# Graph attention, Mamba and relation stages: relation rows, x1, x3 and the routing in another order

## What is computed

```
x = x + attention(layernorm(x), adj)        # masked softmax over s1[i] + s2[j], leaky relu
x = x + mamba2(layernorm(x))                # W_in, conv of 4 taps, 8 heads, W_out, W_lin
x = x + relation(layernorm(x), adj)         # sum over r of (adj == r) @ x @ weight[r], r = 1..4
x = x + moe(layernorm(x))                   # 8 experts, top 1, capacity 1.25 T / E, in token order
```

## Time and profile before

| | |
|---|---|
| median of 3 runs | 3693.07 us (3690.87 to 3696.62) |
| profiled execution | 3692.86 us, span 3691.1 us |
| busy, share of the span | PE 94%, DVE 69%, ACT 47%, POOL 49% |
| mean granted clock of PE | 0.985 of full |
| 100 to 2580 us (rounds) | PE busy 2311.57 us, DVE 1979.52, ACT 1378.12, POOL 1242.03 |
| 2660 to 3691 us (experts) | PE busy 1014.32 us of 1031 |

### The profile page before, as it was taken

The page is one execution under the profiler, slowest core; times in us unless marked ns, Lnnn a source line. Parts: engine busy times, 40 slices in busy tenths (PEclk is TensorE's granted clock), DMA queues, the critical chain, the costliest instruction groups (busy, mean ns, idle before and its releaser), DMA issues.

```text
span 3691.1 us, 63266 instructions
## 1 busy us (share of the span) xinstructions
PE 3452.6 (94%) x19340; PEld 2780.1 (75%) x19340; DVE 2537.9 (69%) x7375; ACT 1743.9 (47%) x3691; POOL 1807.0 (49%) x2010
## 2 busy tenths in 40 slices
PE   7999999999999999999999999999699999999998
PEld 6777777777777777777777777767488888888887
DVE  4877878787787878878778778787444444444444
ACT  3555555565565555556555555555223232323232
POOL 2455545445455454554545455454345454545453
PEclk8999999999999999999999999999799999999999
DMA  3111211111121111111112121111155555555553
GB/s 118 38 39 46 36 36 40 43 37 41 42 37 38 40 40 37 46 37 37 40 37 42 35 49 35 36 40 33 51 191 198 193 197 193 196 194 195 195 194 129
DMA packets 168177, 304.60 MB, mean 83 GB/s; under 512 B 38016, under 2 KB 140416, under 8 KB 149952
## 3 DMA queue, kind: packets, MB, share of 16 engines
q0 software_dynamic: 38272, 196.98, 15.4%
q1 hardware_dynamic: 92896, 72.41, 6.4%
q10 hardware_dynamic: 36960, 34.62, 6.2%
HBM read 250.77 MB, written 53.17 MB: 82 GB/s over the span
## 4 chain that ended last, share of the span: by engine, by line
PE 53%; DVE 25%; POOL 12%; issue 9%; ACT 1%; DVEq 0%; DMA 0%; ACTq 0%; POOLq 0%; SPq 0%
PE bank L1398 13%; PE bank L1412 13%; PE bank L1133 7%; POOL masks L482 6%; DVE conv L827 6%; PE bank L1149 5%; PE bank L1237 4%; PE bank L1350 4%; DVE y L1009 3%; POOL row L468 2%; DVE y L1014 2%; POOL rstd L468 2%; DVE stats L808 2%; DVE xn L818 1%; PE bank L1268 1%
## 5 line engine op out<-in xcount | busy, mean ns | idle before, releaser
L748 ACT ACTIVATE decay<-bank,w_up 128x256 f32<-128x256 f32 x568 | 268.8, 473 | 699.9 <-PE bank L1398 699.9
L1133 PE MATMUL bank<-xn1T,w_in 128*128 128x256 f32 x2304 | 524.9, 381 | 11.2 <-issue 9.4
L1149 PE MATMUL bank<-w_rel,hT 128*128 128x264 f32 x2048 | 506.7, 391 | 0.0
L1398 PE MATMUL bank<-zs,w_up 128*128 128x256 f32 x2272 | 503.5, 380 | 0.6 <-ACT zs L607 0.6
L1412 PE MATMUL bank<-w_dn,decay 128*128 128x256 f32 x2272 | 502.1, 379 | 0.0
L1133 PEld LDWEIGHTS bank<-xn1T,w_in 128*128 128x128 f32 x2304 | 431.6, 190 | 71.9 <-issue 12.0
L827 DVE SCALAR_TENSOR_TENSOR conv<-bank,conv_w,conv 128x255 f32<-128x255 f32 (+2 forms) x960 | 461.2, 480 | 34.8
L1398 PEld LDWEIGHTS bank<-zs,w_up 128*128 128x128 f32 x2272 | 432.7, 190 | 60.0 <-issue 0.9
L1412 PEld LDWEIGHTS bank<-w_dn,decay 128*128 128x128 f32 x2272 | 426.2, 190 | 55.1
L1081 DVE TENSOR_TENSOR hT<-bank,w_dn 128x256 f32<-128x256 f32 x142 | 60.3, 425 | 535.9 <-PE bank L1412 535.9
L1149 PEld LDWEIGHTS bank<-w_rel,hT 128*128 128x128 f32 x2048 | 369.2, 190 | 73.3 <-ACT hT L607 13.0
(11 more groups left out here) (238 smaller groups left out, 6189.7 us busy)
## 6 DMA issues: line engine op xcount, KB each, us to landing
token_rows<-row SPq DMA_DIRECT2D x64, 266.0 KB, 2.8
xT_sb<-in_xT ACTq DMA_DIRECT2D x64, 256.0 KB
x_sb<-in_x ACTq DMA_DIRECT2D x64, 256.0 KB, 2.7
adj_sb<-in_adj SPq DMA_DIRECT2D x64, 256.0 KB, 3.0
adjt_sb<-in_adjT SPq DMA_DIRECT2D x64, 256.0 KB, 3.0
out<-row SPq DMA_DIRECT2D x64, 256.0 KB, 2.2
w_in<-token_rows,idc POOLq DMA_INDIRECT x142, 4.7
out<-hT,ids POOLq DMA_INDIRECT x142, 2.4
```

Of the source, the lines that this page charges most:

```text
L748: nc.scalar.activation(hid(f), bank[f % 4][:, 0:GROUP], ACT.Relu, bias=b1[q % 2][:, f:f + 1]).then_inc(hid_ready, 1)
L1133: ins = mm(dst, w_in[:, k, first:first + P], xn1T[:, k, :], start=k == 0, stop=k == DK - 1)
L1149: ins = mm(bank[6 + t][:, 0:GX], hT[:, d, r * N + t * P:r * N + (t + 1) * P], w_rel[:, r, d, :], start=r == 0 and d == 0, stop=r == R - 1 ...
L1398: ins = mm(bank[f % 4][:, 0:GROUP], w1[i][:, k, f * P:(f + 1) * P], xgT[:, k, :], start=k == 0, stop=k == DK - 1)
```

## The change

Five things are done, all in the rounds.

1. PE: for t = 1, only the third relation stays ahead of L1333, behind `expo` of heads 4 to 7; the fourth comes behind L1333, and gy_made with it. L1322 moves ahead of `expo` of heads 4 to 7, and both `attend` of the next batch move ahead of L1333.
2. DVE: x1 and its deviation stand between the second and the third weighing.
3. DVE: x3 moves behind y, with its deviation and (behind x2) the logits. POOL makes the power for x1 before the fourth mask and that for x3 behind the sums of y's squares.
4. A group is routed in the first round of the next group instead of the last round of its own: `route` is cut into best_expert, between x3 and its deviation, and slots, at the end of the round. `place` scatters four tiles in the round after.
5. The last two batches are one group; its routing stands behind the last round.

```diff
-    GROUPS = NB // GB + 1
+    GROUPS = NB // GB
...
-        def routed(g):
+        def to_route(turn_):
+            if turn_ is None or turn_[1] != 0 or is_first(turn_[0]):
+                return None
+            return turn_[0] - 1
...
-                            place(g_ - 1, sum(share[:i]), sum(share[:i + 1]))
...
                     gp.tensor_scalar(noedge[:], adj[:], 0.0, NEG_BIG, ALU.is_le, ALU.mult).then_inc(noedge_ready, 1)
+                if turn_ is not None and turn_[1] == 1 and not is_first(turn_[0]):
+                    place(turn_[0] - 1)
...
                     edge_masks(0, R - 1)
-                if b3_ is not None:
-                    rsqrt(3, b3_)
+                if b1_ is not None:
+                    rsqrt(1, b1_)
                 if b2_ is not None:
                     edge_masks(R - 1, R).then_inc(masks_ready, 1)
-                if b1_ is not None:
-                    rsqrt(1, b1_)
...
                     gp.tensor_tensor(y2s[:], y2h[:, 0, :], y2h[:, 1, :], ALU.add).then_inc(y2s_ready, 1)
+                if b3_ is not None:
+                    rsqrt(3, b3_)
                 if b2_ is not None:
                     rsqrt(4, b2_)
...
                     weigh(range(0, 2), b2_)
-                if b3_ is not None:
-                    dve.wait_ge(gy_made, b3_ + 1)
...
-                    ins = v.tensor_tensor(row[:, :, 0:GX], bank67[:, :, 0:GX], x2b[:], ALU.add)
...
-                    deviation(3, row[:, :, 0:D], ch4, b3_)
-                if b2_ is not None:
-                    weigh(range(2, 4), b2_)
                 if b1_ is not None:
...
                     deviation(1, x1, ch1b, b1_)
...
+                if b2_ is not None:
+                    weigh(range(2, 4), b2_)
...
                 if b3_ is not None:
-                    g_, i, n = turn_
-                    if i == n - 1:
-                        dve.wait_ge(lg_in, b3_ + 1)
-                        route(g_, n * T)
+                    dve.wait_ge(gy_made, b3_ + 1)
...
+                    ins = v.tensor_tensor(row[:, :, 0:GX], bank67[:, :, 0:GX], x2b[:], ALU.add)
+                    ins.then_inc(x3_ready, 1)
+                g_ = to_route(turn_)
+                if g_ is not None:
+                    best_expert(g_)
+                if b3_ is not None:
+                    dve.wait_ge(x3_ready, b3_ + 1)
+                    deviation(3, row[:, :, 0:D], ch4, b3_)
...
                     deviation(2, x2, ch3, b2_)
...
+                    ins.then_inc(lg_in, 1)
+                if g_ is not None:
+                    slots(g_)
 
             rounds(dve, step)
+            best_expert(GROUPS - 1)
+            slots(GROUPS - 1)
...
                     expo(range(0, 4), b2_)
-                if b3_ is not None:
-                    relate(1, range(2, R)).then_inc(gy_made, 1)
-                if b2_ is not None:
-                    expo(range(4, H), b2_)
...
                     ins.then_inc(hp_made, 1)
+                if b2_ is not None:
+                    expo(range(4, H), b2_)
+                if b3_ is not None:
+                    relate(1, range(2, 3))
+                if b1_ is not None and not is_last(b1_):
+                    attend(0, b1_ + 1)
+                    attend(1, b1_ + 1).then_inc(wh_made, 1)
...
                             ins.then_inc(y_made, 1)
-                if b1_ is not None and not is_last(b1_):
-                    attend(0, b1_ + 1)
-                if b1_ is not None and not is_last(b1_):
-                    attend(1, b1_ + 1).then_inc(wh_made, 1)
+                if b3_ is not None:
+                    relate(1, range(3, R)).then_inc(gy_made, 1)
...
+                g_ = to_route(turn_)
+                if g_ is not None:
+                    pe.wait_ge(x3_ready, b3_ + 1)
+                    count(g_)
```

More of the change, by code:

```diff
@@ L468, in rsqrt, with place @@
                 gp.tensor_tensor(rstd[i][:], ve[i][:], mhalf[:], ALU.pow).then_inc(rstd_ready[i], 1)
-            def place(g, first, last):
+            def place(g):
                 pool.wait_ge(slot_ready, g + 1)
                 carry(pool)
-                for t in range(first, last):
+                for t in range(GT):
                     gp.indirect_dma_start(
@@ L545, in _ @@
             rounds(pool, step)
-            place(GROUPS - 1, 0, T)
+            place(GROUPS - 1)
             def fetch_up(n):
@@ L728, in step @@
                                              ACT.Square).then_inc(y2_ready, 1)
[L729 to L732, removed]
+                g_ = to_route(turn_)
+                if g_ is not None:
+                    gate_exponents(g_)
             rounds(act, step)
+            gate_exponents(GROUPS - 1)
             def turn(n):
@@ new lines, in best_expert @@
+                three = lambda a: a[:].unsqueeze(2).broadcast_to([P, GT, E])
+                chr_.start()
+                dve.wait_ge(lg_in, GB * g + GB)
+                lk(v.tensor_reduce(lmax[:], lg[:], AX.X, ALU.max))
+                v.tensor_tensor(lg2[:], lg[:], three(lmax), ALU.subtract).then_inc(lg_ready, 1)
+                dve.wait_ge(ge_ready, g + 1)
+                v.tensor_reduce(gsum[:], ge[:], AX.X, ALU.add)
+                lk(v.tensor_reduce(gmax[:], ge[:], AX.X, ALU.max))
@@ new lines, in best_expert @@
+                v.reciprocal(grec[:], gsum[:])
+                lk(v.tensor_tensor(eq[:], ge[:], three(gmax), ALU.is_equal))
+                v.tensor_tensor(prb[:], gmax[:], grec[:], ALU.mult)
+                lk(v.tensor_tensor(rv[:], eq[:], rev[:], ALU.mult))
+                lk(v.tensor_reduce(rmax[:], rv[:], AX.X, ALU.max))
+                need(dve, cum_made, g)
+                v.tensor_tensor(ohb[:], rev[:], three(rmax), ALU.is_equal).then_inc(oh_ready, 1)
+                v.tensor_tensor(oh[:], rev[:], three(rmax), ALU.is_equal)
@@ L884, in step @@
             def step(b1_, b2_, b3_, turn_):
-                for chain in (ch1, ch1b, ch2, ch3, ch4, chr_):
+                for chain in (ch1, ch1b, ch2, ch3, ch4):
                     chain.start()
@@ L1033, in step @@
                     deviation(2, x2, ch3, b2_)
+                if b3_ is not None:
+                    if is_first(b3_):
+                        dve.wait_ge(rel_in, 16 * len(rel_loads))
+                    dve.wait_ge(rstd_ready[3], b3_ + 1)
+                    for t in range(T):
+                        ins = v.scalar_tensor_tensor(lg[:, T * turn_[1] + t, :], row[:, t, D:GX], row[:, t, GX + 1:GX + 2],
+                                                     gate_b[:, t, :], ALU.mult, ALU.add)
+                    ins.then_inc(lg_in, 1)
+                if g_ is not None:
+                    slots(g_)
             rounds(dve, step)
+            best_expert(GROUPS - 1)
+            slots(GROUPS - 1)
             lk = lambda ins: chp.link(dve, ins, 0)
@@ L1151, in relate, with count @@
                 return ins
+            def count(g):
+                pe.wait_ge(oh_ready, g + 1)
+                mm(bank[7][:, 0:E], triub[:], ohb[:, 0, :], start=True, stop=True)
+                mm(bank[7][:, E:(GT + 1) * E], onesb[:], ohb[:, 0:1, :].broadcast_to([P, GT, E]), start=True,
+                   stop=False, skip_group_check=True)
+                mm(bank[7][:, E:GT * E], triub[:], ohb[:, 1:GT, :], start=False, stop=False, skip_group_check=True)
+                for j in range(1, GT):
+                    ins = mm(bank[7][:, (j + 1) * E:(GT + 1) * E], onesb[:],
+                             ohb[:, j:j + 1, :].broadcast_to([P, GT - j, E]), start=False, stop=j == GT - 1,
+                             skip_group_check=True)
+                ins.then_inc(cum_made, 1)
             def expo(heads, b):
```

117 lines of the change are left out of this document (41 added, 76 removed).

## The result

The changed kernel takes 3610.47 us (median of 4 runs, 3608.35 to 3616.02) against 3691.97 (4 runs, 3686.05 to 3696.62): a ratio of 0.9783, with a 95% interval from 0.9768 to 0.9797. The profiled execution took 3608.35 us.

The account below looks back on a forecast made before the run. PE was taken to bound the rounds, with 2.7 us of stall each; a pair falls from 80.1 to 77.5 us, times 31 is 81; 3692.9 - 81 + 2 = 3614, clock -10 and +11, forecast 3615, range 3585 to 3660.

Parts of the forecast that it names:

- The unrouted turn: Rounds, prob transposes B to A: PE leads and the turn takes 37.3 us.
- DVE's 0.2 us to spare: Unrouted turn: DVE needs 37.1 us against PE's 37.3, so PE leads with 0.2 us to spare.
- The routed turn: Rounds, prob transposes A to B: DVE's chain from y leads and takes 40.2 us, 1.3 more than before.
- Waits of PE: PE in the rounds: L1128's wait gone, L1350's under 15 us, L1142's 5 to 25, L1237's about 50.
- the cover for y: PE, end of the relation rows: the last quarter, run to 10.9 us, covers the wait for DVE's y.
- The power of x1: POOL beside the weighings: rstd1's power takes near 1.4 us.
- Rival 2: Routed turn: x3 moves eq and rv off POOL's sums, locks vanish, pair 76.3 us, time 3577; chance 0.12.
- the 10 forecast: PE's clock in the rounds: existing drops cost 7 x 1.7 = 12 us, most go with the stalls, -10 us.
- the +11 for new drops in routed rounds: PE before L1237: the new gap of 2 us brings clock drops in every second routed round, +11 us.
- Rival 4: PE's clock: the new gap before L1237 drops it, 1.7 us each; in every round, about 3718; chance 0.07.
- Four scatters: POOL in B behind noedge: four scatters, 5.8 us, fit its 9.10 us of idle time before x2b.
- +2: End of the rounds: +2.9 us for four scatters before the final wait, about 1 gained on y, net +2.

Follow-up runs that it names:

- the late spare work: Changed kernel plus two spare statistics on DVE at the end of the step, behind slots: 3631.61 us in routed rounds only, 3620.92 us in unrouted rounds only.
- the early power: Changed kernel with the variance and power of y's squares ahead of x3's in routed rounds: 3567.63 us; with the last relation quarter also ahead of `attend`: 3549.28 us.
- the quarter: Changed kernel with the fourth relation's rows of the second token tile back ahead of the next batch's `attend`: 3600.62 us, ratio 0.9760.
- x1 behind: Changed kernel with x1 and its statistics back behind all four weighings, and both `attend` behind the products of the decays: 3722.61 us, ratio 1.0094.
- the early spare work: Changed kernel plus two spare statistics on DVE right behind x3's statistics: 3614.35 us in routed rounds only, 3615.81 us in unrouted rounds only.

## Why the prediction was right, and where it was not

The forecast was 3615; 3610.47 was measured, and the two turns, 40.21 and 37.40, are those of the sum (40.2 and 37.3). The mechanism held, in particular which engine leads which turn; several terms were off and met by luck. Point by point:

**The unrouted turn.** Every step came 0.4 to 0.8 us later than counted, and the end did not. From L1313 at 1932.97: `attend` 5.92 (5.45 forecast), L1356 7.94 (7.3), xn1's transposes 11.69 (10.9), w_proj 12.13 (11.3), L1378 16.16 (15.5 in A, 15.8 in B), next masks 25.36 (25.3), next prob 37.41 (37.3). Two errors met, by luck. x1 is later than I counted: beside the masks two weighings took 2.31 us here, not 1.81, and `attend` waits 0.45. The sum had 0.1 for that wait, and named up to 0.4 for a weighing held by a mask; it is 0.45 in nearly every unrouted turn, not now and then. The other way, I had set the loop's branch at 0.5, and L1378 to the masks is 9.20 with it, not 9.5. DVE's 0.2 us to spare is borne out by the late spare work (0.25).

**The routed turn.** y ends at 12.2 (12.3 forecast), x3 and best_expert take 4.32 (4.0), statistics and two powers 2.71 (2.75), x2 to the end of the taps 7.90 (8.05), taps to prob 13.12 (13.1), which makes 40.2. That DVE leads here is shown by the early power (1.46 us less), and up to the masks' product by the late spare work as well.

**Waits of PE.** As forecast: none at xn1, 1.1 us at y (under 15), 12.6 at `attend` (5 to 25), 54.3 at the masks' product (about 50), y2s named before the sum. Before prob it is 0.59 rather than 1.0.

**The quarter, wrong.** The step was "The last quarter of the relation rows runs to 10.9 and is the cover for y." y needs no cover: in the changed kernel ACT's squares and POOL's sums behind the copy of xn1T decide when L1378 starts, and the same paragraphs named that chain. With the quarter ahead of `attend`, L1376 starts 0.51 us earlier in the unrouted turn (15.65 for 16.16), and the turn takes 36.93 instead of 37.40. I took the quarter as given and did not ask what the other place would give.

**The power of x1.** 1.4 was forecast; it is 1.38 at 1940.11 and 0.97 in the rounds on either side (1899.79, 1977.39), each beside DVE's weighings, and each ends 0.58 us behind the weighing that was under way.

**The locks.** Rival 2, that they vanish, did not come: eq 0.84 and rv 0.72 stand in the changed kernel. They went where best_expert ran with POOL idle. With the quarter ahead of `attend` other operations meet the sums: eq takes 0.47, rv 0.18, and prb between them 0.74 (0.16 in the changed kernel).

**Clock.** The seven drops of 1.7 us from 100 to 2560 us became two in the same rounds (at 440 and 1843), 8.5 us less for the 10 forecast; the +11 for new drops in routed rounds did not come. That was in part luck: five experiments with the same wait of 1.82 us ahead of the masks' product had six or seven drops behind it. Rival 4 was nearer than its 0.07 says, for 0.6 us more of wait brought a drop in every routed round. Its price was too high, since a drop there lengthens the turn by only 0.40 us: the rest lies under DVE's lead.

**Head and tail.** Four scatters fit into POOL's idle time: x2b follows an idle time of 3.63 us. For the end I had +2; it is -2.7. PE in the last rounds, after:

```profile
2478.26 0.66 PE L1313 MATMUL bank<-identf,prob 128*128 128x128 f32 x4 [0.34 <-ACT prob L707]
...
2527.24 0.61 PE L1378 MATMUL bank<-ones_row,y2s 128*128 128x1 f32 x4
...
2554.44 0.17 PE L1162 MATMUL bank<-ohb,triub 128*128 128x8 bf16 x1 [5.42 <-DVE ohb L857]
...
2570.08 0.69 PE L1392 MATMUL bank<-identf,x2b 128*128 128x128 f32 x2 [15.34 <-DVE x2b L1065]
...
2579.16 1.19 PE L1412 MATMUL bank<-zs,w_up 128*128 128x256 f32 x2 [0.56 <-ACT zs L604]
```

Before, the same five starts are 2559.99, 2616.97, 2643.43, 2655.37 and 2664.44. From the last prob to the last sum of squares it went from 56.98 to 48.98 us, to the last count +0.7, to the expert's first transposes +3.7 (+2.9 forecast, for the scatters), from there to L1412 0, and +0.8 in the rest. The mis-sized term is the first: I counted 1 us for one last round, and there are two of them, and the kernel before also had half clock in this stretch, 3.4 us of it lost at 2571 and 1.7 at 2613.

The 4.2 us ahead of the 61 turns were not forecast and go with PE's clock at the start of the program. Up to the third transposing of prob the granted clock is at half for 34.1 us in the kernel before and 23.9 in the changed one, which is 5.1 us of full clock. Two experiments with equal code up to there differ in the same way: 107.8 us with 34.1 at half (late spare work, unrouted) and 103.5 with 23.9 (routed). The other runs with equal code up to there, all with 23.9 us or less at half, took 104.0 to 105.8. Why the clock comes up later in some executions stays open.

So the whole is 84.4 us less where the sum had 78: 77.6 for 80 in the turns and their clock, 4.2 for nothing ahead of them, and 2.7 less for 2 more behind them.

## What to carry to other kernels

When a stall is removed, name the chain that is late next and put moved work where the waiting engine waits for something else, not in front of that chain: the quarter fills a wait at one place and costs 0.2 to 0.5% at the other. An engine's idle time is only free if nothing behind it is late; spare work put at several places of a step tells which idle time is free and who leads. On a chain that leads, order small producers by who is waited for first: one power moved past another gave 1.2%. Before a result with spare work is read, look at how much it delays what follows: 0.8 us here delayed it by 0.47 to 0.62.

## What the hardware did that I had not expected

- PE's clock falls behind waits shorter than I had thought, and not each time. From 100 us to the end of the rounds, a wait of 1.82 us ahead of the masks' product, once in two rounds, was followed by a drop to half in 2 of 30 cases in the changed kernel, and in 6 or 7 in the five experiments that kept it (the quarter, x1 behind, the early spare work twice, the late one in unrouted rounds). One of 2.04 us ahead of `attend` was followed by a drop in 12 of 30, one of 2.42 in all 30, and one of 0.6 (both runs with the early power) in none. Each drop lost 1.7 us; with 5.55 us nearly each pair lost 3.4. Whether the length of the wait decides or the moment at which it comes, no run here separates. The loss outlasts the wait and falls on the products behind it.
- DVE and POOL hold each other in more places than eq and rv, and not in the same way both ways. By the single instructions of the changed kernel from 100 to 2450 us, a weighing (two SBUF inputs) that is under way holds POOL: each of 58 powers beside one ends 0.58 us behind it, and each of 31 masks that start 0.1 us behind one takes 2.2 us instead of 1.5 and ends 1.35 us behind it. A weighing that starts together with a mask takes 1.43 us instead of 0.95 and ends 0.06 to 0.08 us ahead of the mask (33 cases; this is the 2.31 us above), but one that starts 0.5 us into a mask is not held (0.96 at 1935.43). The exclusive lock does not describe that last case; what does, no run here shows.
- Beside one of POOL's masks (1941.58) the two normalisations of xn1 took 1.02 us, where they take 0.73 with POOL idle (at 1967.44 in the kernel before), though they have one tile as input. What holds them, no run here shows.
